# Layer 0 of a convolution and attention kernel: patches and taps loaded as single transfers to 128 partitions, base rows in DRAM by half of the array, row and channel

## The reference

```python
base = _conv1x1(x, w_qkv)                            # 192 -> 576 channels
qkv = jnp.concatenate([_dwconv(base, w_dw3, 1), _dwconv(base, w_dw5, 2), _dwconv(base, w_dw7, 3)], axis=1)
qkv = _conv1x1(qkv, w_pconv)                         # 1728 -> 576 channels
q, k, v = jnp.split(qkv, 3, axis=1)
# ... normalised q and k, attention over channels in 8 heads, three masked softmaxes, projection
```

## Time and profile before

| | |
|---|---|
| median of 3 executions | 2520.53 us |
| the profiled execution | 2517.25 us |
| its span, first to last instruction | 2515.5 us |
| mean granted TensorE clock | 0.883 |
| TensorE matmul busy | 1945.1 us (77%) |
| VectorE busy | 1287.4 us (51%) |
| ScalarE busy | 804.7 us (32%) |
| GpSimd busy | 870.2 us (35%) |
| DMA, mean over the span | 169 GB/s |
| HBM read, written | 299.33 MB, 121.96 MB |

### The profile page before, as it was taken

One profiled execution on the slowest core, in us unless ns is written; L12 is line 12 of the kernel. 1 busy time (PEld: TensorE's weight loads), 2 busy tenths in 40 slices (PEclk: granted clock), 3 DMA queues, 4 the chain that ended last, 5 costly groups with the idle time before them and its releaser, 6 DMA issues. The chain is left out here.

```text
span 2515.5 us, 36893 instructions
## 1 busy us (share of the span) xinstructions
PE 1945.1 (77%) x15660; PEld 1203.3 (48%) x15660; DVE 1287.4 (51%) x1313; ACT 804.7 (32%) x1269; POOL 870.2 (35%) x459
## 2 busy tenths in 40 slices
PE   3879779769999999999978768777777777774052
PEld 1577666667777777777734322222222222221031
DVE  6445444441111111111271166799999999988803
ACT  3445445440000000000122125633543533335410
POOL 3334233220000000000000040599899899983300
PEclk9889899889999999999988778899899979987555
DMA  7899999988131313130120040678688868863799
GB/s 197 249 311 314 316 292 304 296 257 241 59 118 59 118 60 118 60 118 1 43 59 11 0 139 21 156 197 219 171 213 216 209 175 213 218 179 90 224 215 294
DMA packets 195538, 424.51 MB, mean 169 GB/s; under 512 B 18733, under 2 KB 143661, under 8 KB 184717
## 3 DMA queue, kind: packets, MB, share of 16 engines
q1 hardware_dynamic: 182540, 414.81, 58.8%
q10 hardware_dynamic: 12832, 7.34, 1.1%
HBM read 299.33 MB, written 121.96 MB: 167 GB/s over the span
## 5 line engine op out<-in xcount | busy, mean ns | idle before, releaser
L743 PE MATMUL ps<-mem 128*128 128x288 f16 x5376 | 654.6, 287 | 14.4 <-DMA mem<-depthwise_out 14.4
L743 PEld LDWEIGHTS ps<-mem 128*128 128x128 f16 x5376 | 502.1, 98 | 152.9 <-issue 15.4
L1717 POOL TENSOR_TENSOR mem<-mem 128x1024 f32<-128x1024 f32 x192 | 465.7, 2444 | 45.3 <-ACT mem L1651 42.9
L1626 PE MATMUL ps<-mem 128*128 128x512 f32 x768 | 417.9, 676 | 39.1 <-POOL mem L1717 35.0
L1112 POOL TENSOR_TENSOR mem<-mem 128x1536 f16<-128x1536 f32 x16 | 50.8, 3180 | 940.3 <-ACT mem L1090 940.3
L533 PE MATMUL ps<-mem 56*96 56x240 f16 (+1 forms) x5184 | 308.2, 280 | 86.1 <-DMA mem<-base_phases 53.0
L533 PEld LDWEIGHTS ps<-mem 56*96 56x96 f16 x5184 | 297.7, 128 | 111.4 <-DMA mem<-base_phases 58.5
L786 DVE TENSOR_TENSOR mem<-ps,mem 128x128 f16<-128x128 f32 x64 | 18.7, 292 | 586.8 <-ACT mem L807 586.8
L1746 DVE TENSOR_TENSOR_SCAN mem<-mem,ps 128x1024 f32<-128x1024 f32 x132 | 307.8, 2332 | 18.2 <-issue 10.3
L646 DVE TENSOR_TENSOR mem<-ps,mem 96x1024 f16<-96x1024 f32 x144 | 175.3, 1220 | 217.9 <-ACT mem L578 217.9
L1626 PEld LDWEIGHTS ps<-mem 128*128 128x128 f32 x768 | 153.5, 213 | 242.9 <-issue 134.5
(11 more groups left out here) (202 smaller groups left out, 1915.4 us busy)
## 6 DMA issues: line engine op xcount, KB each, us to landing
mem<-l_bc SPq DMA_DIRECT2D x504, 256.0 KB, 4.5
depthwise_out<-mem SPq DMA_DIRECT2D x105, 512.0 KB, 9.4
mem<-depthwise_out SPq DMA_DIRECT2D x31, 1664.0 KB, 10.8
mem<-base_phases SPq DMA_DIRECT2D x72, 448.0 KB
base_phases<-mem SPq DMA_DIRECT2D x56, 512.0 KB, 9.9
mem<-in_wd SPq DMA_DIRECT2D x72, 336.0 KB
mem<-l_planes SPq DMA_DIRECT2D x48, 252.0 KB
mem<-in_x SPq DMA_DIRECT2D x4, 2048.0 KB, 13.6
```

The source lines that it names most:

```text
L743: ins = nc.tensor.matmul(ps[:, 2 * (i % 2) + h, 0:HALF], d, pw[rows, wa, k, HALF * h:HALF * h + HALF], start=(k == 0 and n == 0), stop=(k ...
L1626: ins = nc.tensor.matmul(py[:, a, :], ident, hh[:, n % 4, 512 * a:512 * a + 512], start=(n % N == 0), stop=(n % N == N - 1))
L1717: nc.gpsimd.tensor_tensor(hh[:, n % 4, :], hh[:, n % 4, :], cs[:, n % 4, :], ALU.mult).then_inc(hc_pool, 1)
```

## The change

It changes where the data lie in DRAM and with how many transfers they move. Nothing that a compute engine works out changes.

- `base_phases` goes from `[56, 576, 512]` to `[2, 64, 288, 512]`: half of the array, row, channel within the half. A patch batch is then one transfer to 128 partitions. Rows 56 to 63 of each half are unused; six new transfers write zeros from the cleared `ext` into them once, at the end of `first_loads` (L406 of the new kernel), and POOL's first shift and SP's first patch load wait until they have landed.
- The taps get 64 rows per half (zero rows among them), so a batch is one transfer to 128 partitions, and the three clears of `w32` go. The clear of `ext` moves to POOL's front.
- The base weights are permuted, so that each base tile has the first half's channels on its lower and the second half's on its upper partitions; every base store is split into two stores of 64 partitions (32 for the last m).
- x is laid out by the host as `[128, 3, 4096]` (`x_rows`). The third part loads as two transfers to 128 partitions on SP; ACT's two transfers go.

```diff
-        base_d = nc.dram_tensor("base_phases", [TAPROWS, QKV, PITCH0], F16).ap()
+        base_d = nc.dram_tensor("base_phases", [2, 64, QKV // 2, PITCH0], F16).ap()
...
-                    sp.dma_start(xt[:, t, :], x_dram[t, 0:128, :]).then_inc(loaded[t], 16)
+                    sp.dma_start(xt[:, t, :], x_dram[:, t]).then_inc(loaded[t], 16)
...
-                    sp.dma_start(xt[0:64, 2, s], x_dram[0, 128:192, s]).then_inc(rest_loaded[h], 16)
+                    sp.dma_start(xt[:, 2, s], x_dram[:, 2, s]).then_inc(rest_loaded[h], 16)
...
-            if x_dram is not None:
-                for h in range(2):
-                    s = slice(HW // 2 * h, HW // 2 * (h + 1))
-                    act.dma_start(xt[64:128, 2, s], x_dram[1, 128:192, s]).then_inc(rest_loaded[h], 16)
...
-        for t in range(2):
-            sp.dma_start(w32[n % NTB][64 * t:64 * t + TAPROWS], inp["wd"][TAPROWS * t:TAPROWS * (t + 1), n * BP * TAPS0:(n + 1) * BP * TAPS0]
-                         ).then_inc(w_loaded[n % NTB], 16)
+        sp.dma_start(w32[n % NTB], inp["wd"][:, n * BP * TAPS0:(n + 1) * BP * TAPS0]).then_inc(w_loaded[n % NTB], 16)
 
     def first_loads(sp):
         sp.dma_start(w, inp["wbase"]).then_inc(base_loaded, 16)
-        sp.wait_ge(taps_cleared, NTB)
         for n in range(NTB):
             load_taps(sp, n)
+        sp.wait_ge(ext_cleared, 1)
+        for t in range(2):
+            for k in range(3):
+                sp.dma_start(base_d[t, TAPROWS:64, 96 * k:96 * k + 96].rearrange("r c n -> c r n"),
+                             ext[0:96, 0:2].rearrange("c a r n -> c (a r) n")).then_inc(rest_stored, 16)
 
     def clear(pool):
-        for k in range(NTB):
-            nc.gpsimd.memset(w32[k][32:64], 0.0).then_inc(taps_cleared, 1)
-        pool.wait_ge(taps_cleared, NTB)
+        nc.gpsimd.memset(ext.rearrange("p s r n -> p (s r n)").bitcast(F32), 0.0).then_inc(ext_cleared, 1)
...
-        nc.gpsimd.memset(ext.rearrange("p s r n -> p (s r n)").bitcast(F32), 0.0).then_inc(ext_cleared, 1)
...
+            def base_rows(m, t, row):
+                return base_d[t, row:row + 4, 64 * m:64 * m + width(m) // 2].rearrange("r c n -> c r n")
+
+            def half(v, m, t):
+                return v[width(m) // 2 * t:width(m) // 2 * (t + 1)]
...
-                sp.dma_start(base_d[4 * g:4 * g + 4, 128 * m:128 * m + width(m)].rearrange("r c n -> c r n"),
-                             stb[0:width(m), j % NSTB]).then_inc(base_stored[j % NSTB], 16)
+                for t in range(2):
+                    sp.dma_start(base_rows(m, t, 4 * g), half(stb[:, j % NSTB], m, t)).then_inc(base_stored[j % NSTB], 16)
...
-                    sp.dma_start(base_d[row:row + 4, 128 * m:128 * m + width(m)].rearrange("r c n -> c r n"),
-                                 ext[0:width(m), SHIFTED.index(g)]).then_inc(ext_stored[SHIFTED.index(g)], 16)
+                    for t in range(2):
+                        sp.dma_start(base_rows(m, t, row), half(ext[:, SHIFTED.index(g)], m, t)).then_inc(ext_stored[SHIFTED.index(g)], 16)
...
-                slot, c0 = n % NWIN, 2 * BP * n
-                for t in range(2):
-                    sp.dma_start(win[64 * t:64 * t + TAPROWS, slot], base_d[:, c0 + BP * t:c0 + BP * t + BP]).then_inc(win_loaded[slot], 16)
+                src = base_d.rearrange("t r c n -> (t r) c n")[:, BP * n:BP * n + BP]
+                sp.dma_start(win[:, n % NWIN], src).then_inc(win_loaded[n % NWIN], 16)
...
             wait_stored(0)
+            sp.wait_ge(rest_stored, 96)
...
-            pool.wait_ge(ext_cleared, 1)
+            pool.wait_ge(rest_stored, 96)
```

More of the change, by code:

```diff
@@ L239, in _ @@
                     if t == 2 and k % 4 == 0:
-                        dve.wait_ge(rest_loaded[k // 4], 32)
+                        dve.wait_ge(rest_loaded[k // 4], 16)
                     last = nc.vector.bn_stats(stats[:, t * 8 + k, :], xt[:, t, 512 * k:512 * k + 512])
@@ L326, in layer0_depthwise @@
     ext_cleared = sem("l0_shifted_cleared")
+    rest_stored = sem("l0_unused_rows_stored")
     ext_done = sem("l0_base_shifted")
     ext_stored = [sem("l0_shifted_stored") for _ in SHIFTED]
-    sem.shifted = (ext_stored, 16 * NM)
+    sem.shifted = (ext_stored, 32 * NM)
     base_sum = sem("l0_base_in_psum")
@@ L416, in clear @@
                 nc.gpsimd.memset(wh[k][:, a * WB:a * WB + WB + MD * a].bitcast(F32), 0.0).then_inc(taps_cleared, 1)
-        nc.gpsimd.memset(ext.rearrange("p s r n -> p (s r n)").bitcast(F32), 0.0).then_inc(ext_cleared, 1)
-    rs, nb = group_norm(nc, sem, norm_at, ps, inp, 0, ident, raw, x_dram=xin, apply=False, more_sp=first_loads, more_pool=clear)
+    rs, nb = group_norm(nc, sem, norm_at, ps, inp, 0, ident, raw, x_dram=inp["x_rows"], apply=False, more_sp=first_loads, more_pool=clear)
     def by_phase(t, g):
@@ L544, in _ @@
                     if k == 0:
-                        pe.wait_ge(win_loaded[n % NWIN], 32 * (n // NWIN + 1))
+                        pe.wait_ge(win_loaded[n % NWIN], 16 * (n // NWIN + 1))
                         pe.wait_ge(w_hi, NTAP * (n + 1))
@@ L556, in base @@
                     if b == 0 and j >= NSTB:
-                        act.wait_ge(base_stored[j % NSTB], 16 * (j // NSTB))
+                        act.wait_ge(base_stored[j % NSTB], 32 * (j // NSTB))
                         act.wait_ge(ext_done, shifts_to((j - NSTB) // 8, (j - NSTB) % 8))
@@ L561, in taps @@
             def taps(n):
-                act.wait_ge(w_loaded[n % NTB], 32 * (n // NTB + 1))
+                act.wait_ge(w_loaded[n % NTB], 16 * (n // NTB + 1))
                 if n >= 2:
@@ L565, in taps @@
                 else:
-                    act.wait_ge(taps_cleared, NTB + 2 * (n + 1))
+                    act.wait_ge(taps_cleared, 2 * (n + 1))
                 src, dst = dense_taps(n)
@@ L608, in shift @@
                     if m:
-                        pool.wait_ge(ext_stored[SHIFTED.index(g)], 16 * m)
+                        pool.wait_ge(ext_stored[SHIFTED.index(g)], 32 * m)
                     src, dst = grid(stb[0:width(m), (8 * m + g) % NSTB]), grid(ext[0:width(m), SHIFTED.index(g)])
@@ L2035, in layouts @@
     o = {"x": v["x"], "ident": np.eye(128, dtype=f)}
+    x = v["x"].reshape(B, C, HW)
+    o["x_rows"] = np.stack([x[0, 0:128], x[1, 0:128], np.concatenate([x[0, 128:192], x[1, 128:192]], 0)], 1)
     def packed_rows(w):
@@ L2046, in layouts @@
     wq = v["L0_conv_w_qkv"].T
-    o["wbase"] = np.stack(packed_rows(wq), 1)
+    tiles = [np.arange(m, min(m + 128, QKV)).reshape(-1, 2, BP).transpose(1, 0, 2).reshape(-1) for m in range(0, QKV, 128)]
+    o["wbase"] = np.stack(packed_rows(wq[:, np.concatenate(tiles)]), 1)
     dws = [v["L0_conv_w_dw3"][:, 0], v["L0_conv_w_dw5"][:, 0], v["L0_conv_w_dw7"][:, 0]]
-    wd = np.zeros((2, TAPROWS, QKV // 2, TAPS0), f)
+    wd = np.zeros((2, 64, QKV // 2, TAPS0), f)
     place = {(1, q, ro): 32 * q + 8 * ro for q in range(3) for ro in range(4)}
@@ L2062, in layouts @@
                     wd[t, n, :, place[o_, q, ro] + po] = dws[q].reshape(-1, 2, BP, *dws[q].shape[1:])[:, t, :, dy + k, dx + k].reshape(-1)
-    o["wd"] = wd.reshape(2 * TAPROWS, QKV // 2 * TAPS0)
+    o["wd"] = wd.reshape(128, QKV // 2 * TAPS0)
     pT = v["L0_conv_w_pconv"].T
```

4 lines of the change are left out of this document (2 added, 2 removed).

## The result

The changed kernel takes 2505.72 us (median of 20 executions, 2496.82 to 2521.59), the kernel before beside it 2520.89 us (20 executions, 2511.9 to 2528.45). The ratio is 0.9948, with a 95% interval of 0.9934 to 0.9963: 15 us faster. Predicted were 37 us less, 2484 us. The direction and the range held, the size did not. The profiled execution took 2503.95 us (span 2502.1, granted clock 0.89), 13.3 us less than that of before.

The account below looks back on a forecast made before the run. Transfers, not PE, were taken to bind the depthwise stage. Head 3, first patches 2, three groups 28 and fourth group 4 made 37 us less: 2480 against the profiled execution, 2484 us against the median; range 2462 to 2522.

Parts of the forecast that it names:

- the same 8%: Depthwise groups: summed transfers before, 114 us, were 8% above the measured groups, so 90.4 us after was scaled to 84.
- PE's own floor for a group: Eight depthwise batches: 13.5 us per base batch, 7.9 or 10.7 per plain one, 94.0 us; 96 us taken per group.
- 28 + 4 us: Gain in the depthwise groups: 28 us from the first three (ends 0 and 34), 4 from the fourth (0 and 8).
- the chain: Plain batch after plain batch: taps start on ACT after unit 1's eviction, through POOL to PE; 2.8 us wait each.
- The head: x load and norm block before the depthwise stage: block ends at 36.5 us instead of 39.88, 3 us less.
- The first patches: First patch load, from SP's issue to PE's start: wide load takes 2.6 us instead of 4.4; 2 us less taken.
- the halves: Base stores split into 64-partition stores: costed at nothing, by the m = 4 stores' stretch at 364 GB/s.
- Fit into the 28 us: Head: the 14 base stores of m = 0, 22 us, fit between the first base sum and the last.
- Half the gain: First rival: mixed transfers and low clock keep depthwise groups near 101 us; 17 to 20 us less, 2502 us; chance 0.18.
- The slower one, the halves: Second rival: 64-partition base stores go at half rate, 168 GB/s; 32 us more, 2552 us; chance 0.05.
- A ceiling on the total: Third rival: DRAM limits the depthwise groups to 302 to 313 GB/s, so added bytes cost time; 2545 us; chance 0.04.

Follow-up runs that it names:

- after_taps: Changed kernel with only the taps of batch n+1 made after unit 0 of batch n, not unit 1: 2492.34 us, ratio 0.9890.
- a_nobase: `a_zeros` without the base stores of m = 1 to 4, patches read from the rows of m = 0: 2490.88 us, ratio 0.9883.
- a_taps_act: `a_actload` with the taps of batch n+1 made after unit 0 of batch n, not unit 1: 2476.13 us, ratio 0.9818.
- a_taps: `a_zeros` with the taps of batch n+1 made after unit 0 of batch n, not unit 1: 2484.83 us, ratio 0.9851.
- b_taps: Kernel before with only the taps of batch n+1 made after unit 0 of batch n, not unit 1: 2508.08 us, ratio 0.9954.
- b_rows: Kernel before with each base store cut into two stores of two rows on all 128 partitions: 2524.81 us, ratio 1.0023.
- a_out96: `a_zeros` with a batch's output stored as one transfer of 96 partitions instead of three of 32: 2495.84 us, ratio 0.9902.
- a_zeros: Changed kernel with the zeros written by 2 transfers of 128 long rows instead of 6: 2504.46 us, ratio 0.9945.
- a_actload: `a_zeros` with the patch loads of batches 2 to 35 issued on ACT's queue after unit 0: 2496.48 us, ratio 0.9908.
- a_pairs: `a_zeros` with the base stores of two steps merged into one of 8 rows per half: 2503.55 us, ratio 0.9944.
- b_x: Kernel before with only x laid out on 128 partitions: 2509.95 us, ratio 0.9956.
- a_nobase_taps: `a_nobase` with the taps of batch n+1 made after unit 0 of batch n, not unit 1: 2443.66 us, ratio 0.9686.

## Why the prediction was off

**Two bounds of a group, both too low.** The prediction said "By the same 8% the transfers of a group after are 90.4 / 1.08 = 84 us" and "PE's own floor for a group is 4 x 13.5 + 7.9 + 3 x 10.7 = 94.0 us". The runs show 99.1 us for the first (`after_taps`, chain gone) and 101.9 to 102.4 for the second (`a_nobase`, base stores gone). The changed kernel's mean is 101.5; neither is a hard floor: two of its groups took 99.4 and 99.5, with the clock up in some of their plain batches, and `a_taps_act` moves the bytes of a group in 96.6. I gave the groups 28 + 4 us; 14.3 came. Of the 23.7 us missing from the profiled executions, 17.7 lie here, 5.5 between the start and the first group, and the rest behind. At 99.1 us a group the transfers alone would have left 24 of the 32 (420.4 - 4 x 99.1), at 102 the chain alone 12. Lifting the chain quickens the kernel before as well, so the change is worth no more without it (15.7 us). With cheap zeros too it is 26 of the 37. The other 11 are open; that they are the transfers' is likely, since PE still waits 38 us for patches in `a_taps`, and `a_taps_act`, with these loads on another queue, is 34 us under `b_taps` by the ratios.

**The transfers.** My sum gave each kind its own rate and added them. A group moves 4 x 5.24 + 4 x 3.41 = 34.6 MB; in 84 us that is 412 GB/s, more than any kind reached alone in the earlier trace rows. In truth it moves at 334 (after) to 350 (`a_taps_act`), with the share at 0.99 to 1.00. The 8% by which the sum missed the kernel before was no error of scale to carry over: it put that kernel at 114 us, 8% above what it took, and this one at 90.4, 9% below the 99.1. The same sum erred both ways, and dividing by 1.08 made the second error larger. The plain check was at hand: the mix moved at 302 to 313 GB/s before, and the 84 us ask for 412. What holds a mix of wide loads and stores under 350 GB/s isn't settled. The number and width of stores have a part in it (`b_rows` +6 us, `a_out96` 9 us under `a_zeros`), the queue that the patch loads stand in perhaps another (`a_actload` 8 us under it); the base stores of `a_pairs`, merged, none that can be measured.

**The chain and the clock.** The sum took 10.7 us for a plain batch, though the earlier trace rows has 12.06 (270.75 to 282.81), and I named the slower matmuls and left them out of the floor. With the 12.06 the sum is 98 us, with `a_nobase`'s 13.4, 102.

**The head.** The x layout did what was said, and more: 11 us alone (`b_x`), since there nothing holds the block's end (30.12 us against 39.88). In the change the six stores of zeros held SP to 35.16 us; 36.5 was predicted for the block's end and 35.61 measured. The first patches came 4.8 us after their issue instead of 6.8, the 2 us predicted. Missing from the sum was the cost of the halves in the head: I costed 64 partitions at nothing, by the m = 4 stores, and they went at 257 GB/s instead of 337. The 406 GB/s that it also had for 64 partitions come from stores issued in turn from the lower and the upper half (L1912), so both halves can have been under way at once. Why the halves of a base store, issued in such pairs too, lose all the same is not shown. "Fit into the 28 us" was wrong: of the 5 us for head and patches 1.6 remained at PE's first depthwise matmul, and none at the first group.

**The fourth group** was read one batch short; it took 104.6 us and went to 99.4, 5 us as against 4 predicted, right by luck.

**The rivals.** "Half the gain" came nearest, 2502 against 2505.7, with groups of 101 us against 101.5, and named the cause: base batches by the transfers, and the clock low after gaps (half of them, not each). The slower one, the halves, was right in its place and wrong in its size: 250 GB/s stays above the 218 from which it decides. Its price was also added up wrongly: it takes 6 us a group off for the plain batches, where its own 3.0 us a batch make 12, so its 32 us more would be 8. A ceiling on the total of 302 to 313 GB/s is refuted by the 334 of this stage. In the Trainium skill, "DMA: Bandwidth & Descriptors", section "Where 436 GB/s comes from", a ceiling of about 358 GB/s stands between HBM and SBUF. The trace does not agree for loads alone: x came at 426 and 418 GB/s (5 to 9 and 9 to 14 us):

```profile
5.00:9.00 4.00, 0.00 (x0) 0.00 (x0) 0.69 (x2) 0.00 (x0) 4.00 (x5) 1.00 1.00 426
9.00:14.00 5.00, 0.00 (x0) 0.00 (x0) 4.96 (x10) 0.00 (x0) 1.03 (x1) 1.00 0.98 418
```

The mixed traffic of the stage, though, never left 288 to 362 GB/s in any group that was read of a kernel with all its stores.

## What to carry to other kernels

When transfers bind, take the rate of the mix (bytes of a stage over its time, at a DMA share near 1) as the starting point; here rates of kinds measured alone added up to a time that no mix reached. Before counting a gain down to the next floor, price that floor from a whole batch in the timeline, gap and slower matmuls after it included, and look for a second floor just beside it: against `a_zeros`, the base stores away gave 14 us (`a_nobase`), the chain away 20 (`a_taps`), and both away 61 (`a_nobase_taps`), far more than the sum. A one-line move of the taps to an earlier unit, with the patch loads on another queue, took 28 us off `a_zeros` (to 2476.1 us), nearly twice what the change gave.

## What the runs showed of the hardware

- In `a_nobase`, behind each gap of 2.77 us between the plain batches of its first three groups, PE's granted clock fell to the 1.2 GHz level for some 6 us (0.75 and 0.71 over the batches), and 144 matmuls took 10.6 to 10.9 us; behind gaps of 0.9 us (`a_nobase_taps`) it stayed at 1.00 and they took 7.74. In the changed kernel four of eight such gaps had no effect (7.74 us at 507.63).
- Stores of 1024-byte rows from 64 partitions moved 250 to 257 GB/s, from 128 partitions 327 to 337. Of 64 partitions with larger stores (`a_pairs`) 265.
- SP took 26.11 us to issue six stores of 96 partitions by 8 rows of 1024 bytes; two stores of the same zeros with long rows took 4.83 us and let it go at 13.9 us, and the block ends 5.5 us sooner. Whether the number of the stores or of their rows holds it was not separated.
- A lead won in the head need not reach the end: 5.5 us of it were worth 1 us with the chain in place (`a_zeros` against the changed kernel) and 7.5 us without (`a_taps` against `after_taps`), each known to some 6 us. Whether the chain swallows it was not settled.
